# End of the experts: routed rows of the last block and the first norm on GpSimd, another order of the last tiles

## The reference, cut to what matters

```python
def _L1_ffn_ref(hidden_states, ...):
    x = hidden_states.reshape(-1, Hd)
    shared = jnp.einsum('ts,sh->th', jax.nn.silu(x @ sw_gate) * (x @ sw_up), sw_down)
    ...
    routed = jnp.einsum('eth,te->th', expert_out, combine)
    shared_out = jax.nn.sigmoid(x @ shared_gate_w)[:, None] * shared
    return (routed + shared_out).reshape(B, S, Hd)
...
x = _layernorm(x + _L1_ffn_ref(x, ...), axis=-1)
```

## Time and profile before

| what | us |
|---|---|
| median of 3 runs | 955.1 |
| lowest, highest | 954.23, 955.57 |
| the profiled execution | 953.87 |
| its span, first to last instruction | 951.8 |
| busy in the span: PE, DVE, ACT, POOL | 866.0, 702.3, 687.0, 261.3 |

### The profile page before, as it was taken

One profiled execution on the slowest core, in us unless ns is written; L12 is line 12 of the kernel. 1 busy time (PEld: TensorE's weight loads), 2 busy tenths in 40 slices (PEclk: granted clock), 3 DMA queues, 4 the chain that ended last, 5 costly groups with the idle time before them and its releaser, 6 DMA issues.

```text
span 951.8 us, 20997 instructions
## 1 busy us (share of the span) xinstructions
PE 866.0 (91%) x7200; PEld 711.0 (75%) x7200; DVE 702.3 (74%) x2130; ACT 687.0 (72%) x1538; POOL 261.3 (27%) x360
## 2 busy tenths in 40 slices
PE   3777899999999998999999999999998998999994
PEld 2556778788888887676777776767666987899994
DVE  6888878878875557888888989898987462365447
ACT  2778857768676337999999999999998322366646
POOL 0345542322343120200202021111112256334432
PEclk8889999999999999999999999999999999999998
DMA  6203021110010012010202020202021212244534
GB/s 200 67 1 98 15 79 62 40 35 13 13 45 13 24 34 61 21 28 1 70 2 70 1 70 2 69 1 59 10 66 48 86 62 94 73 109 124 133 136 174
DMA packets 54760, 54.85 MB, mean 58 GB/s; under 512 B 17953, under 2 KB 48929, under 8 KB 54658
## 3 DMA queue, kind: packets, MB, share of 16 engines
q1 hardware_dynamic: 51250, 44.18, 16.0%
q0 software_dynamic: 3408, 9.34, 2.8%
HBM read 32.85 MB, written 20.65 MB: 56 GB/s over the span
## 4 chain that ended last, share of the span: by engine, by line
PE 50%; DVE 19%; ACT 18%; issue 8%; DMA 2%; POOL 1%; another core or an unknown queue 1%; DVEq 0%; ACTq 0%; SPq 0%; POOLq 0%
PE ps L445 11%; PE ps L447 9%; PE ps L446 9%; PE ps L969 5%; ACT G L1492 4%; ACT G L1502 4%; ACT wu_rows L1492 3%; PE ps L986 3%; PE ps L957 2%; PE ps L677 2%; PE ps L692 2%; DVE G L2037 2%; ACT RT L1252 1%; PE ps L750 1%; DVE wu_rows L2037 1%
## 5 line engine op out<-in xcount | busy, mean ns | idle before, releaser
L1492 ACT ACTIVATE G<-G,small 128x256 f32<-128x256 f32 x296 | 133.7, 517 | 7.0 <-DVE small L2037 7.0
L445 PE MATMUL ps<-WU 128*128 128x256 f32 x384 | 117.4, 306 | 17.3 <-DVE wu_rows L1859 6.7
L2037 DVE CUSTOM_DVE_ANT_0 G<-ps,nb 128x256 f32<-128x256 f32 x296 | 111.6, 419 | 20.7 <-PE ps L957 17.8
L1502 ACT COPY G<-ps 128x512 f32<-128x512 f32 x192 | 113.3, 590 | 9.6 <-PE ps L969 9.5
L2398 POOL TENSOR_SCALAR_AFFINE_SELECT G<-G 128x256 f32<-128x256 f32 x128 | 76.3, 619 | 145.8 <-ACT G L1337 145.6
L446 PE MATMUL ps<-WU 128*128 128x256 f32 x384 | 108.7, 283 | 0.0
L447 PE MATMUL ps<-WU 128*128 128x256 f32 x384 | 108.6, 283 | 0.0
L1492 ACT ACTIVATE wu_rows<-wu_rows,small 128x256 f32<-128x256 f32 x216 | 98.1, 518 | 3.2 <-DVE small L2037 3.2
L969 PE MATMUL ps<-ident,G 128*128 128x128 f32 x592 | 92.6, 283 | 4.6 <-ACT G L1502 3.3
L2037 DVE CUSTOM_DVE_ANT_0 wu_rows<-ps,nb 128x256 f32<-128x256 f32 x216 | 81.6, 419 | 14.6 <-PE ps L957 13.4
L445 PEld LDWEIGHTS ps<-WU 128*128 128x128 f32 x384 | 73.1, 190 | 25.8 <-DVE WU L1865 9.5
(11 more groups left out here) (251 smaller groups left out, 2354.5 us busy)
## 6 DMA issues: line engine op xcount, KB each, us to landing
xs<-G SPq DMA_DIRECT2D x8, 645.0 KB, 6.5
G<-xs SPq DMA_DIRECT2D x39, 128.0 KB
G<-x SPq DMA_DIRECT2D x17, 256.0 KB, 3.4
G<-in_x SPq DMA_DIRECT2D x16, 256.0 KB, 2.8
wu_rows<-yy SPq DMA_DIRECT2D x8, 512.0 KB, 7.6
x<-G SPq DMA_DIRECT2D x15, 256.0 KB, 2.4
wu_rows<-in_wu SPq DMA_DIRECT2D x8, 384.0 KB, 5.7
wraw<-in_wu SPq DMA_DIRECT2D x8, 256.0 KB, 2.9
```

What stands on the lines that cost most here:

```text
L445: pe.matmul(o, lh, rh, start=start, stop=False, skip_group_check=True)
L1492: m = act.activation(p, p, ACT.Exp, scale=-1.0, bias=mneg[:, k:k + 1])
L1502: act.copy(probT(h), halves(2 + h % 2)).then_inc(probT_act, 1)
L2037: m = dve.tensor_tensor_reduce(prob(H2 * i + h)[:, t, :], ps[:, SCORE_BANKS[(H2 * i + h) % 3], S * t:S * (t + 1)], nbv[:, t, :], 1.0, -FMI ...
```

## The change

On VectorE `add_routed` becomes `add_first` and `add_second` for blocks 0 to 2; block 3's two adds go to GpSimd (128x1024 each, semaphore pool_rows), and VectorE waits for them ahead of the shared rows. Block 2's adds move from after tile 22 to between the last low halves. On ScalarE silu(23) comes after hidden_hi(22), the table load ahead of hidden_hi(23), the squares of blocks 1 and 2 after hidden_hi(23); norm3(0) goes to GpSimd as four TENSOR_SCALAR instructions. SP loads the routed rows in the order of blocks 0, 3, 1, 2, and stores blocks 0, 1, the halves of 3, and 2. Apart from this, one semaphore at the start of the kernel is folded into another (the waits count 16 more).

```diff
--- before.py
+++ after.py
@@ -372,7 +372,7 @@
-        LAST_NORM = 12 + 2 * BLOCKS3 + 1
+        LAST_NORM = 12 + 2 * (BLOCKS3 - 1) + 1
@@ -502,8 +502,8 @@
             for j in range(2, RAW1):
                 raw_load(j)
             sp.wait_ge(diag_ready, 1)
-            sp.dma_start(ediag, diagonals).then_inc(diag_stored, 16)
-            sp.wait_ge(diag_stored, 16)
+            sp.dma_start(ediag, diagonals).then_inc(skewed, 16)
+            sp.wait_ge(skewed, 16)
             for t in range(2):
                 skew = bass.AP(ediag.tensor, S - P * (t + 1), [[1, P], [1, S]])
                 sp.dma_start(skewed_bias[:, S * t:S * (t + 1)], skew).then_inc(skewed, 16)
@@ -615,18 +615,19 @@
                 sp.dma_start(meta[:, i, :], xs[tile, E:ROW]).then_inc(tile_loaded[i % 3], 16)
             for n in range(3):
                 sp.wait_ge(y_sent[n], 16 * (SLOT_TILES // 3))
-            for b in range(BLOCKS3):
+            for b in (0, BLOCKS3 - 1, 1, 2):
                 for c in range(2):
                     sp.dma_start(Y[b][c], block_rows(yy, b, T * c)).then_inc(y_loaded[b], 16)
             b = BLOCKS3 - 1
-            for at in range(b):
-                if at == b - 1:
-                    sp.wait_ge(x_combined, LAST_NORM)
-                    sp.dma_start(rows(out, 2 * b, 2), XO[b][:, 0:2, :]).then_inc(stored[3], 16)
-                sp.wait_ge(xo_ready, NORMS[3] + at + 1)
-                sp.dma_start(block_rows(out, at), XO[at]).then_inc(stored[3], 16)
-            sp.wait_ge(x_combined, LAST_NORM + 1)
-            sp.dma_start(rows(out, 2 * b + 1, 2), XO[b][:, 2:4, :]).then_inc(stored[3], 16)
+            sp.wait_ge(pool_rows, 3)
+            sp.dma_start(block_rows(out, 0), XO[0]).then_inc(stored[3], 16)
+            sp.wait_ge(xo_ready, NORMS[3] + 1)
+            sp.dma_start(block_rows(out, 1), XO[1]).then_inc(stored[3], 16)
+            for t in range(2):
+                sp.wait_ge(x_combined, LAST_NORM + t)
+                sp.dma_start(rows(out, 2 * b + t, 2), XO[b][:, 2 * t:2 * t + 2, :]).then_inc(stored[3], 16)
+            sp.wait_ge(xo_ready, NORMS[3] + 2)
+            sp.dma_start(block_rows(out, 2), XO[2]).then_inc(stored[3], 16)
             sp.wait_ge(stored[3], 16 * (BLOCKS3 + 1))
 
 
...
-                pe.wait_ge(skewed, 32)
+                pe.wait_ge(skewed, 48)
@@ -1632,15 +1633,18 @@
                 scale_out(SLOT_TILES - 2)
                 silu(before)
                 scale_out(SLOT_TILES - 1)
-                for n in range(before + 1, 4 * SH_TILES):
+                end = 4 * SH_TILES - 1
+                for n in range(before + 1, end):
                     silu(n)
                     hidden_hi(n - 1)
-                    if before + 3 <= n < before + 5:
-                        squares3(n - before - 3)
-                hidden_hi(4 * SH_TILES - 1)
-                squares3(BLOCKS3 - 2)
+                    if n == before + 3:
+                        squares3(0)
+                hidden_hi(end - 1)
+                silu(end)
                 act.activation(small[:, 321:322], eps_col, ACT.Sqrt)
-                norm3(0)
+                hidden_hi(end)
+                squares3(1)
+                squares3(2)
                 norm3(1)
                 b = BLOCKS3 - 1
                 act.wait_ge(var_ready, NORMS[3] + b + 1)
@@ -2221,16 +2225,16 @@
                         dve.wait_ge(block_moved[b], 2 * BY_CHOICE)
                     add_shared(n, Z[b][:, E * t:E * (t + 1)]).then_inc(x_combined, 1)
 
-                def add_routed(b):
+                def add_first(b):
 
                     dve.wait_ge(y_loaded[b], 32)
-                    if b < BLOCKS3 - 1:
-                        dve.wait_ge(x_combined, 4 * b + 4)
+                    dve.wait_ge(x_combined, 4 * b + 4)
                     rows_b3 = X[:, 4 * b:4 * b + 4, 0:E]
-                    step(x_combined, 12 + 2 * b + 1, dve.tensor_tensor(rows_b3, rows_b3, Y[b][0], ALU.add))
-                    if b == BLOCKS3 - 1:
-                        step(x_combined, 12 + 2 * b + 2, dve.tensor_tensor(rows_b3, rows_b3, Y[b][1], ALU.add))
-                        return
+                    dve.tensor_tensor(rows_b3, rows_b3, Y[b][0], ALU.add).then_inc(x_combined, 1)
+
+                def add_second(b):
+
+                    dve.wait_ge(x_combined, 12 + 2 * b + 1)
                     for t in range(4):
                         row = X[:, 4 * b + t, 0:E]
                         m = dve.tensor_tensor_reduce(row, row, Y[b][1][:, t, :], 1.0, 0.0, ALU.add, ALU.add, row_sum[b][:, t:t + 1])
@@ -2293,17 +2297,24 @@
                     if 4 <= i < 16:
                         add_kept(i - 4)
                 hg_low(SLOT_TILES - 1)
-                for n in range(before, 4 * SH_TILES):
+                end = 4 * SH_TILES - 1
+                for n in range(before, end):
                     product(n)
                     if n > before:
                         hidden_lo(n - 1)
                     b = n - before - 2
-                    if 0 <= b < BLOCKS3 - 1:
-                        add_routed(b)
+                    if 0 <= b < 2:
+                        add_first(b)
+                        add_second(b)
                         means(b)
-                hidden_lo(4 * SH_TILES - 1)
+                product(end)
+                hidden_lo(end - 1)
+                add_first(2)
+                hidden_lo(end)
+                add_second(2)
+                means(2)
                 b = BLOCKS3 - 1
-                add_routed(b)
+                dve.wait_ge(pool_rows, 2)
                 for t in range(4):
                     if t % 2 == 0:
                         dve.wait_ge(down_done[3], 4 * SH_TILES + t // 2)
@@ -2536,8 +2547,19 @@
                 pool.wait_ge(y_scaled, i + 1)
                 at = meta[:, i, 1:2].bitcast(U32)
                 pool.indirect_dma_start(yy, bass.IndirectOffsetOnAxis(ap=at, axis=0), yo[i % 3], None).then_inc(y_sent[i % 3], 16)
-            for b in range(BLOCKS3 - 1):
-                layernorm3(b)
+            last = BLOCKS3 - 1
+            pool.wait_ge(y_loaded[last], 32)
+            rows_b3 = X[:, 4 * last:4 * last + 4, 0:E]
+            for c in range(2):
+                pool.tensor_tensor(rows_b3, rows_b3, Y[last][c], ALU.add).then_inc(pool_rows, 1)
+                pool.wait_ge(pool_rows, c + 1)
+            layernorm3(0)
+            pool.wait_ge(rstd_ready, NORMS[3] + 1)
+            for t in range(4):
+                m = pool.tensor_scalar(XO[0][:, t, :], X[:, t, 0:E], rstd3[0][:, t:t + 1], shift3[0][:, t:t + 1], ALU.mult, ALU.add)
+            m.then_inc(pool_rows, 1)
+            layernorm3(1)
+            layernorm3(2)
 
 
 # ---- launch: one core; the host only lays the inputs out ----
```

More of the change, by code:

```diff
@@ L355, in program @@
                  "probT_act probT_dve mixed2 ident_ready fixed_ready consts aw0_raw aw0_raw_rest aw0_hi aw0_ready vp_ones "
-                 "rel_loaded rel_step diag_row diag_ready diag_stored skewed bias_turned "
+                 "rel_loaded rel_step diag_row diag_ready skewed pool_rows bias_turned "
                  "bias_ready router_loaded router_hi router_ready raw_ready raw_free split_w_hi split_w passed "
@@ L362, in program @@
          probT_act, probT_dve, mixed2, ident_ready, fixed_ready, consts, aw0_raw, aw0_raw_rest, aw0_hi, aw0_ready, vp_ones,
-         rel_loaded, rel_step, diag_row, diag_ready, diag_stored, skewed, bias_turned,
+         rel_loaded, rel_step, diag_row, diag_ready, skewed, pool_rows, bias_turned,
          bias_ready, router_loaded, router_hi, router_ready, raw_ready, raw_free, split_w_hi, split_w, passed,
```

## The result

The changed kernel takes 957.8 us (median of 13 runs, 955.7 to 963.7) against 954.2 us for the kernel before (median of 13, 952.6 to 955.9). The ratio is 1.0041, with a 95% interval of 1.0027 to 1.0055: 3.9 us slower, 2.6 to 5.2 (the two medians alone differ by 3.6). The forecast was 2.6 us more, with a range that reaches to 4.9 us above the median that it started from. That median of 3 runs was 955.1, and over 13 runs it is 954.2; so the forecast time of 957.7 agrees with the measured 957.8 partly by luck, and the difference is what has to be compared.

A forecast was written before the change was run, and what follows sets the result against it. VectorE's and ScalarE's queues end level; the wait (2.42 us), hold (2.37) and reordered last tiles, against 2.51 us of removed adds, put the last issue 2.65 us later: 955.1 + 2.6 = 957.7 us, range 954.4 to 960.0.

The forecast's parts named there:

- Where the end is: Tail: VectorE hands over its statistics at 945.01, ScalarE starts the last norm at 945.97; the two queues end level.
- The wait for block 1: VectorE, after block 0: block 1's rows, now loaded third, land at 932.50, so it stands 2.42 us from 930.08.
- The hold: VectorE's block 1 adds: GpSimd's second add of block 3 holds them through the memory port, 2.37 us.
- my two cases: Block 1's adds: VectorE's first add goes first and fused adds wait until 936.1, or GpSimd first, all wait until 935.0.
- the first rival: Block 1's fused adds on VectorE are not held by GpSimd's add: +0.4 us, 955.5; chance 18%.
- The last tiles: VectorE from tile 22's product at 937.74: shared adds start at 944.6, 3.1 us later, including 0.4 for GpSimd's normalisations.
- The table load: ScalarE, before tile 23's high half: the early load, 939.5 to 941.0, costs nothing; without cover it would cost 1.5.
- TensorE's clock: Gap before tile 21's down product grows to 4.6 us; half clock for one of three products costs 0 to 0.9.
- Landing alike: End of span: the last output, issued at 951.0 against 948.34, takes as long to land as before.

The follow-up runs named there:

- relief of ScalarE alone: Kernel before with the semaphore edit, table load ahead of tile 23's high half, block 0's norm on GpSimd, new store order: ratio 0.9991 (0.9963 to 1.0018).
- the two runs that only change the order: Load order 0, 3, 1, 2 alone in the kernel before: ratio 1.0026; load order 0, 1, 3, 2 in the changed kernel: 0.9996.
- the two ratios: The changed kernel timed twice against the kernel before, the second time without an edit: 1.0041 (1.0027 to 1.0055) and 1.0052 (1.0036 to 1.0069).
- the run with both edits: Changed kernel with loads in the order 0, 1, 3, 2 and GpSimd's two adds cut to 4 elements per partition: ratio 0.9969 (0.9943 to 0.9996).

## Why the prediction was right

The sign, the two mechanisms and their places came out; the change measured 3.2 us in the profiles and 3.9 us in the times, against 2.6. By its steps:

- **Where the end is.** VectorE's queue sets it, with ScalarE's just beside. Right for the change: relief of ScalarE alone gave 0.85 us of tail and 0.4 to the end, and each delay of VectorE showed up in the tail. With the loads in the order 0, 1, 3, 2 the end was ScalarE's, which stood 1.17 us for GpSimd.
- **The wait for block 1.** Forecast 2.42 us, measured 2.65. The third pair was there 0.46 us later than the third pair before. That is not one execution's spread: in the five profiles with block 3 second the sixth load lands 11.9 to 12.1 us after the first issue, and in the five with blocks 0, 1 and 2 in front 11.4 to 11.7. So block 3's loads are slower, and the forecast gave them the times of block 1's. Block 3 is read in pieces of one row, the others in pieces of four, but no run tests whether that is why. That the price is the place in the queue is shown by the two runs that only change the order.
- **The hold.** Forecast 2.37 us, measured 3.06 - 1.22 = 1.84. The rule held: whole instruction, two inputs in SBUF, turns. The size was off for two reasons: GpSimd's add takes 2.24 us (4.48 for two), not 2.37, and VectorE's wait was longer, so more of the second add fell into it. Of my two cases the one in which GpSimd goes first occurred. The sum of wait and hold, 4.49 us, was forecast as 4.79. Whether the fused form is held, on which the first rival hung, is settled by the run with GpSimd's adds alone: 2.32 and 2.38 us instead of 0.42. By the rule of the Trainium skill named in the prediction ("SBUF — State Buffer", section "Who interferes with whom": the shared port pair is an exclusive lock, and VectorE contends for it when both its inputs are in SBUF and GpSimd reads SBUF) it had to be so. The trace agrees, with these 2.32 and 2.38 us.
- **The last tiles.** Forecast 0.4 us for the normalisations on the path; here they held one low half by 0.05 (0.73 instead of 0.68). In other orders they cost up to 0.7. The silu behind the high half made VectorE wait 0.70: the product of tile 23 starts 1.98 us after that of tile 22, where the forecast had 1.76. The table load was covered, as forecast.
- **TensorE's clock.** The gap was forecast at 4.6 us and measured 4.61; the clock fell; the forecast put the cost at 0 to 0.9 and took none of it into the sum. It is 0.5, and it reached the end by a way that I had not listed, the buffer shared by tiles 21 and 23. This is the term that is missing in the sum.
- **The landing of the last output.** "Landing alike" was wrong by 0.3: the last one is now 512 KB and lands in 3.3 us, against 3.0 for 256 KB in the earlier trace rows.

So the errors are +0.5 (where block 1 starts), -0.5 (hold), +0.2 (silu of tile 23), -0.35 (normalisations), +0.5 (clock) and +0.2 (end of the span): together the 0.6 between forecast and profile, within rounding. The two large ones, where block 1 starts and the hold, were off by half a microsecond each in opposite directions; that the sum is better than its terms is luck. What stays open is the rest between the 3.2 us from the first load to the end of the span and the 3.9 and 5.0 us by the two ratios. No sign of the semaphore edit is in it (1.0007, with 1 in the interval). The first interval, from 2.6 us, holds 3.2, the second begins just above it at 3.4; it may be spread of the executions, but no run shows that.

## What to carry to other kernels

Before work goes from VectorE to GpSimd to relieve it, look at what VectorE does at the same time. If that has two inputs in SBUF, it stands in these runs until GpSimd's instruction is over, and that is longer (2.24 us against 1.25 for the same add) than what was taken off: with GpSimd's adds alone, two holds of 1.9 us for 2.5 us of work. Put such work beside instructions that read PSUM, or into a wait. And when loads are queued together, moving one ahead delays all that it overtakes: ask which consumer has no slack.

## What the runs showed of the hardware that I had not expected

- A gap on TensorE of 2.75 us before the down product of tile 21 brought the granted clock down to 0.50 in the run with the new load order, while gaps of 2.37 to 2.38 us before that of tile 22 did not in four profiles (the earlier trace rows and the runs of the semaphore edit and of ScalarE's relief). But in the kernel before a gap of 2.24 us that ended at 117.0 was followed by a clock of 0.50 (118 to 121). So for gaps of this size the length alone does not tell.
- The same 128x256 TENSOR_SCALAR takes 0.55 us on GpSimd beside PSUM work, 0.67 in the changed kernel, and 1.2 (4.90 for four, in the run with both edits) amid VectorE's adds: GpSimd pays for the collision as well.
- What an output costs depends on what is under way: 256 KB landed in 3.0 us as the last of 1 MB issued within 1.4 us, and in 3.7 as the last of 1.5 MB issued within 1.8. Bringing the last issue forward by 1.3 us gained 0.5.
